# Scan of a four-block model: one saturating add for two state groups, odd groups decayed by GpSimd, block diagonal tables loaded from memory

## The reference, cut to what matters

```
xr, gate = split(x @ W_in.T, 2)                  # 512 channels each
xc = silu(causal_conv(xr + t_emb))               # 4 taps
xn = layernorm(xc) * ln_g + ln_b
Bm, Cm, dt = split(xn @ W_xproj.T, 3)            # 16 states each
Ad = 1 + tanh(dt @ W_dt.T + b_dt) * 0.01 * -tanh(A_log)
Bd = Bm * min(norm(xn), 1)
def step(h, (ad, bd, xt, ct)):                   # h: 16 x 512 for each sequence
    h = clip(h * ad[:, :, None] + bd[:, :, None] * xt[:, None, :], -10, 10)
    return h, einsum('bd,bdh->bh', ct, h)        # y_t
y = scan over the 64 tokens + D * xn
out = (y * silu(gate)) @ W_out.T
```

## Time and profile before

| | |
|---|---|
| median of 3 runs | 1796.69 us (1794.53 to 1799.46) |
| the profiled execution's own time | 1796.37 us |
| its span | 1794.6 us |
| DVE, PE busy | 1623.4 us (90%), 1636.4 us (91%) |
| ACT, POOL busy | 1297.0 us (72%), 622.6 us (35%) |
| attention, both layers | up to about 550 us |
| layer 1: front, scan, post | about 550 to 745, 745 to 1094, 1094 to 1180 us |
| layer 2: scan, post | 1370 to 1718, 1718 to 1794.6 us |

### The profile page before, as it was taken

One profiled execution on the slowest core, in us unless ns is written; L12 is line 12 of the kernel. 1 busy time (PEld: TensorE's weight loads), 2 busy tenths in 40 slices (PEclk: granted clock), 3 DMA queues, 4 the chain that ended last, 5 costly groups with the idle time before them and its releaser, 6 DMA issues. The chain is left out here.

```text
span 1794.6 us, 42356 instructions
## 1 busy us (share of the span) xinstructions
PE 1636.4 (91%) x13764; PEld 703.6 (39%) x13764; DVE 1623.4 (90%) x2452; ACT 1297.0 (72%) x2197; POOL 622.6 (35%) x576
## 2 busy tenths in 40 slices
PE   7999999999999999788888889999997888888898
PEld 3555555555554445222111114544452221111144
DVE  5899999999987999889999998679998899999975
ACT  5655556465646999888999993069897899999910
POOL 0223232232330222265665550002223566555500
PEclk9999999999999999899999999999998999999999
DMA  4000000000002344653555667624345545556668
GB/s 162 1 2 0 1 2 31 2 1 0 1 1 83 139 160 152 192 171 120 183 160 188 218 186 210 229 83 174 127 169 173 178 132 183 158 187 197 189 224 280
DMA packets 126444, 226.56 MB, mean 126 GB/s; under 512 B 35616, under 2 KB 61216, under 8 KB 117536
## 3 DMA queue, kind: packets, MB, share of 16 engines
q1 hardware_dynamic: 125904, 223.30, 37.8%
q10 hardware_dynamic: 432, 1.84, 0.3%
HBM read 141.73 MB, written 83.36 MB: 125 GB/s over the span
## 5 line engine op out<-in xcount | busy, mean ns | idle before, releaser
L1038 ACT ACTIVATE R<-q,Ast 128x512 f32<-128x512 f32 x1008 | 627.2, 708 | 21.8 <-DVE q L2018 16.6
L2018 DVE CUSTOM_DVE_ANT_0 q<-R,PS 128x512 f32<-128x512 f32 x1008 | 611.2, 677 | 19.7 <-ACT R L1038 9.3
L1479 PE MATMUL PS<-xq,Uw 96*128 96x512 bf16 x1024 | 346.2, 394 | 87.5 <-DVE q L2018 73.2
L613 POOL TENSOR_TENSOR Uw<-Ub,rowmask 96x512 bf16<-96x512 bf16 x256 | 335.8, 1346 | 254.4 <-PE PS L1479 254.4
L1492 PE MATMUL PS<-q,Wy 128*32 128x512 f32 x2048 | 285.2, 620 | 0.3
L1479 PEld LDWEIGHTS PS<-xq,Uw 96*128 96x128 bf16 x1024 | 85.5, 97 | 473.9 <-DVE q L2018 396.0
L1152 PE MATMUL PS<-X,Win 128*128 (+1 forms) x456 | 214.7, 608 | 2.2 <-issue 2.1
L1053 PE MATMUL PS<-xn,Wl 128*128 128x512 f32 x384 | 187.7, 613 | 0.7 <-DVE xn L1605 0.7
L1723 DVE SCALAR_TENSOR_TENSOR acc<-xp,Wc,acc 128x512 f32<-128x512 f32 x192 | 134.5, 748 | 2.6
L547 POOL TENSOR_TENSOR ex<-ex,rs 128x1024 f32<-128x1024 f32 x32 | 76.8, 2401 | 164.2 <-DVE rs L1628 164.2
L1152 PEld LDWEIGHTS PS<-X,Win 128*128 128x128 f32 x456 | 82.5, 191 | 95.8 <-issue 95.1
(11 more groups left out here) (159 smaller groups left out, 2492.6 us busy)
## 6 DMA issues: line engine op xcount, KB each, us to landing
xq<-xpart_d SPq DMA_DIRECT2D x384, 192.0 KB
sg_d<-sg SPq DMA_DIRECT2D x16, 1024.0 KB, 5.0
xn_d<-z SPq DMA_DIRECT2D x16, 1024.0 KB, 3.9
y_d<-ys SPq DMA_DIRECT2D x64, 256.0 KB, 3.8
xnp<-xn_d SPq DMA_DIRECT2D x16, 1024.0 KB, 8.1
sgp<-sg_d SPq DMA_DIRECT2D x16, 1024.0 KB, 11.2
xpart_d<-xh SPq DMA_DIRECT2D x16, 512.0 KB, 2.9
xpart_d<-xmi SPq DMA_DIRECT2D x16, 512.0 KB, 3.8
```

The costliest lines, as they stand in the source:

```text
L613: pl.tensor_tensor(Uw[0:XROWS, h, w, :, :, :], Ub[0:XROWS, w, 0:N, ds(s0, CH)].rearrange("p n t -> p t n").unsqueeze(2).broadcast_to([XROW ...
L1038: act.activation(R[:, w, :], q[:, (t + 1) % 2, w, :], ACT.Copy, scale=Ast[:, h, w, t:t + 1]).then_inc(ac_r, 1)
L1479: pe.matmul(PS[:, w, :], Uw[0:XROWS, h, w, t, :, :].rearrange("p b n -> p (b n)"), xq[0:XROWS, hb, w, s8 % XT, :], start=True, stop=True). ...
L2018: v._custom_dve(bass.dve_ops.TENSOR_ADD_SAT, out=q[:, s8 % 2, w, :], in0=R[:, w, :], in1=PS[:, w, :], s0=CLIP, s1=-CLIP).then_inc(dv_q, 1)
```

## The change

Seven edits are made together.

1. **One add for two groups.** DVE's `step` runs over p = 0, 1 and adds groups 2p and 2p + 1 in one 128 x 1024 instruction over two PSUM banks.
2. **Odd groups decayed by GpSimd.** ACT decays the even groups; GpSimd the odd ones, with `tensor_scalar` (`odd_decay`). The add waits for both.
3. **y copies on ScalarE.** `keep_y` leaves DVE for ACT.
4. **B tables from memory.** The three parts of B are stored into `bdiag_d`, a table in memory that was filled with zeros once (12 DMAs of 256 KB in the attention stage), at such offsets that it is block diagonal. `load_x` gets a fourth DMA that brings `Uw` for two steps. GpSimd's `stage` products, `Ub`, `rowmask`, the rows of ones, nine table loads and the table memsets go. K is 72.
5. **B turned in the front.** `store_b` needs tokens on partitions, so PE transposes rB (`turn_b`) and DVE's `split_b` reads it from PSUM.
6. **GpSimd's `last_parts` waits later**: for `row_r` instead of `rB_r`, that is behind DVE's L1860.
7. In the tail the middle part of x goes to ACT (`last_middle`), the low part to GpSimd in halves (`last_half`).

```diff
-                def split_b(it):
+                def split_b(it, src):
                     v.wait_ge(tv_st, it * (TV_STORES * 16) + TV_STORES * 16)
-                    v.wait_ge(rB_r, it + 1)
+                    v.wait_ge(bt_mm, it + 1)
...
                 def step(pi, c2, s8, first):
                     n = c2 * 8 + s8
-                    for w in range(QW):
-                        v.wait_ge(pe_w, pi * (QW * S) + n * QW + w + 1 + W0)
-                        if w % 2 == 0:
-                            v.wait_ge(pe_yq, pi * (2 * S) + n * 2 - 4 + w // 2 + 1 + USED)
...
+                    for p in range(2):
+                        state = q[:, s8 % 2, 2 * p:2 * p + 2, :].rearrange("p w c -> p (w c)")
+                        fed = PS[:, 2 * p:2 * p + 2, :].rearrange("p w c -> p (w c)")
+                        v.wait_ge(pe_w, pi * (QW * S) + n * QW + 2 * p + 2 + W0)
+                        v.wait_ge(pe_yq, pi * (2 * S) + n * 2 - 4 + p + 1 + USED)
...
+                        v.wait_ge(pd_r, pi * RS + n * 2 - 2 + p + 1 + READY)
+                        v.wait_ge(ac_r, pi * RS + n * 2 - 2 + p + 1 + READY)
                         alone(v)
-                        v._custom_dve(bass.dve_ops.TENSOR_ADD_SAT, out=q[:, s8 % 2, w, :], in0=R[:, w, :], in1=PS[:, w, :],
+                        v._custom_dve(bass.dve_ops.TENSOR_ADD_SAT, out=state, in0=R[:, 2 * p:2 * p + 2, :].rearrange("p w c -> p (w c)"), in1=fed,
                                       s0=CLIP, s1=-CLIP).then_inc(dv_q, 1)
...
+                def odd_decay(pi, c2, s8, p):
+                    h, t = s8 // CH, s8 % CH
+                    if t < 2 and p == 0:
+                        pl.wait_ge(pl_a, pi * CHUNKS + c2 * 2 + h + 1)
+                    pl.wait_ge(dv_q, pi * (2 * S) + c2 * 16 + 2 * s8 + p + 1)
+                    alone(pl)
+                    pl.tensor_scalar(R[:, 2 * p + 1, :], q[:, (t + 1) % 2, 2 * p + 1, :], Ast[:, h, 2 * p + 1, t:t + 1], None,
+                                     ALU.mult).then_inc(pd_r, 1)
...
                 def load_x(ps, k):
+                    rows = bdiag_d[ps, 0:GB * DIAG].rearrange("(r f) -> r f", f=S * ROW)
+                    sp.dma_start(Uw[0:XROWS, k % XB, :, :, :, :].rearrange("p t w b n -> p (t w b n)"),
+                                 rows[:, k * (XT * ROW):(k + 1) * (XT * ROW)].unsqueeze(0)
+                                 .broadcast_to([PARTS, GB * PARTS, XT * ROW])).then_inc(xq_in[k % XB], 16)
...
-                    pl.wait_ge(rB_r, it + 1)
+                    pl.wait_ge(row_r, it * 2 + (2 * AT + 3))
...
+                def keep_y(pi, ck, h):
+                    act.wait_ge(pe_yq, pi * (2 * S) + ck * (2 * CH) + 2 * CH + USED)
+                    act.wait_ge(y_out[h], pi * (CHUNKS // 2 * 16) + (ck - h) * 8 + 16)
+                    alone(act)
+                    act.activation(ys[:, h, :], PS[:, 4 + h, :], ACT.Copy).then_inc(ac_y, 1)
...
+                def turn_b(it, dst):
+                    pe.wait_ge(rB_r, it + 1)
+                    pe.transpose(dst, rB[:, :], ident[:, :]).then_inc(bt_mm, 1)
```

More of the change, by code:

```diff
@@ L184, in cond_resid_kernel @@
         late = ExitStack()
+        sb("table_gap", [P, TT * DI + P], where=late)
         pass_tables.append(tables(1, late))
@@ new lines, in last_half, with last_group @@
+                def last_half(it, k, b):
+                    if b == 0:
+                        pl.wait_ge(xmi_r, it * TT + k + 1)
+                        alone(pl)
+                    cols = slice(b * (DI // 2), (b + 1) * (DI // 2))
+                    low = pl.tensor_tensor(xlo[:, k, cols], xr1[:, k, cols], xmi[:, k, cols], ALU.subtract)
+                    if b:
+                        low.then_inc(xlo_r, 1)
+                def last_group(n, p):
+                    it = l * G + G - 1
+                    if n == 19 and p == 0:
+                        pl.wait_ge(xq_st, it * 48 + 48)
+                        alone(pl)
+                    for k, at in enumerate((20, 22, 23, 25)):
+                        if n == at:
+                            last_half(it, k, p)
@@ new lines, in eight @@
+                def eight(ps, c2, first=False, last=False, tail=False):
+                    pi = l * PASSES + ps
+                    for s8 in range(8):
+                        for p in range(2):
+                            if not (first and s8 == 0):
+                                odd_decay(pi, c2, s8, p)
+                            if tail:
+                                last_group(c2 * 8 + s8, p)
+                        if s8 == 0:
+                            if not first:
+                                stage_decay(ps, c2, 1)
+                        elif s8 == 1:
+                            if not first:
+                                stage_outputs(ps, c2, 1)
+                        elif s8 == 4 and not last:
+                            stage_decay(ps, c2 + 1, 0)
+                        elif s8 == 5 and not last:
+                            stage_outputs(ps, c2 + 1, 0)
+                        elif s8 == 5 and ps + 1 < PASSES:
+                            pl.wait_ge(tab_in[1], l * (16 * TABLES) + 16 * TABLES)
+                            alone(pl)
+                            stage_decay(ps + 1, 0, 0, True)
+                            stage_outputs(ps + 1, 0, 0)
+                        elif s8 == 7 and last and ps + 1 < PASSES:
+                            stage_decay(ps + 1, 0, 1, True)
+                            stage_outputs(ps + 1, 0, 1)
```

289 lines of the change are left out of this document (118 added, 171 removed).

## The result

The changed kernel takes 1984.58 us in the median (1970.3 to 1991.09), the kernel before 1796.54 on the same chip: a ratio of 1.1038 with a 95% interval of 1.0995 to 1.1082. It is slower by 188 us, far outside the predicted range of 1728 to 1806, and it went the way of rival B. The profiled execution took 1987.97 us, its span is 1986.2, 191.6 more than before.

The account below looks back on a forecast made before the run. DVE was taken as the bound, ACT nearly full; afterwards PE's loop at 2.51 us a step. Gains of 6 in steady steps, 13 in tails and 3 in front gave 1796.4 - 22 = 1774 us, range 1728 to 1806.

Parts of the forecast that it names:

- rival B: Scan loop add, decay, add: slower by GpSimd's decay, deciding from 0.85 us a decay; about 1850 with 1.16; chance 0.15.
- the price of GpSimd's decay: Scan, odd groups: a decay taken at 0.65 us, nearer to the one-input cast (0.62) than the two-input difference (1.16).
- The loop around the decay: Scan, same pair: add 1.22, hop to GpSimd 0.18, decay, some 0.3 of waits; 1.70 + 0.65 = 2.35 us a step.
- hidden: GpSimd's load in the scan, 1.3 us a step of decays plus 0.15 for staging, was to cost no time.
- rival A: Scan steps: DVE stays the bound or nearly, 2.28 to 2.43 us a step, 1722 to 1757; chance 0.25.
- the sum: Whole kernel: gains of 6 (steady steps), 13 (tails) and 3 (front), 22 us off 1796.4, giving 1774.
- at nothing: Fourth DMA of `load_x` and other side edits: no cost; queue 3.3 us in 5.0, DMA share about 0.7.
- The wide add: DVE in the scan: one 128x1024 add lasts about 1.22 us, pairs start 1.14 apart, a step 2.28.
- PE's loop of 2.51: Hardware loops: PE's order makes a loop over two steps, 4.57 + 0.45 = 5.02, so 2.51 us a step.
- the waits in front of the add: Hardware loops, between PE's input matmul and DVE's add: 0.45 us, bounds 0.21 and 0.55.
- The tails: 24 tail steps of each layer: 76 us instead of 82.8, a gain of 6.5 a layer, 13 in all.
- The front: Bodies before the scan: L1860 falls from 1.28 to 0.35 us, 0.2 a body, 3 us over 14.

Follow-up runs that it names:

- e3: Changed kernel with only group 3 decayed by GpSimd, groups 0 to 2 by ACT; 1958.0 us, ratio 1.090.
- e4: Changed kernel with GpSimd's decay written as a product of two tensors; 1895.0 us, ratio 1.055.
- n1: Changed kernel with all decays on ACT, y copies on DVE and one narrow add a group; 1890.4 us, ratio 1.052.
- b2: Changed kernel with table loads as three DMAs of 24 rows of 4 KB for every two halves, with their own semaphore; 1978.4 us, ratio 1.105.
- n2: Kernel before with one wide add a pair of groups and nothing else changed; 1862.5 us, ratio 1.035.
- f1: n1 with each half's table load as three DMAs of 24 rows of 2 KB, three halves ahead; 1821.8 us, ratio 1.014.
- n3: Changed kernel with GpSimd's decay cut to 64 of 512 columns, the other 448 left undecayed (timing only); 1891.8 us, ratio 1.050.
- b3: n3 with the table loads of b2 (timing only); 1812.7 us, ratio 1.011.
- b4: Changed kernel with b2's table loads and each odd group's decay shared: ACT columns 0 to 191, GpSimd the rest as a product of two tensors; 1840.5 us.
- f2: b4's shared decay split at column 128 (ACT 128 columns, GpSimd 384), with f1's table loads; 1820.9 us, ratio 1.012.
- g1: f1 with last-pass gate and y loads issued one by one, y copies on ACT, columns 256 to 511 of group 3 decayed by GpSimd; 1794.9 us.

## Why the prediction was wrong

**The failed step is the price of GpSimd's decay**, "a decay has one tensor input and a scalar for each partition, which is nearer to the cast, so I take 0.65", with the bounds 0.62 and 1.16. It is 1.56. Both bounds came from other operations of that width, and the upper one was no bound: an operation with a scalar for each partition that the trace did not show cost a third more than the dearest one it did. What rival B's text quotes for one-input work on GpSimd doesn't hold for this form: the cast of this width takes 0.62. The loop around the decay was right to 0.01 us: 1.70 + 1.56 = 3.26, and e3, in which GpSimd is half idle, measured 3.25; for e4 the same sum gives 2.74, measured 2.67. The price also undoes the sentence that GpSimd's load is "hidden": 2 x 1.56 and 0.15 for staging fill 3.25 us by themselves, which in the changed kernel happens to equal the loop. With the true price the prediction's own sum says 208 x (3.25 - 2.54) = 148 us more in the steady steps. Rival B had the place, the mechanism and the point from which it decides (0.85), but its chance of 0.15 and its far end of 1850 hung on the same wrong bound. (In rival A's sum the upper gain is 54 + 16 = 70, not 75.)

**The clock was not in the sum.** The scans grew by 192.6, of which 148 is the step. Most of the other 45 lies where TensorE was at 1.2 GHz, as read from the places where steps are longer than 3.25; no run isolates it. From 1550 to 1830 us that is two thirds of the time, and there PE can fill the step by itself. The starts of two steps in a row from that stretch, 3.68 us apart:

```profile
1702.97 2.35 DVE L2045 CUSTOM_DVE_ANT_0 q<-R,PS 128x1024 f32<-128x1024 f32 x2 [1.32 <-PE PS L1502]
1706.65 2.35 DVE L2045 CUSTOM_DVE_ANT_0 q<-R,PS 128x1024 f32<-128x1024 f32 x2 [1.33 <-PE PS L1502]
```

Between them PE's inputs start at 1705.41, 1.87 after y, and the next y at 1707.22, 1.81 after the inputs: no pause is left. At 2.4 GHz, in the changed kernel, PE pauses some 1.2 us a step (0.94 and 0.31 in front of its inputs of 1001.76 and 1003.67). What pause exactly makes the clock fall isn't settled: from 995 to 1124 us the same steps ran at 2.4 GHz. In e4 and n1 it fell behind waits for transfers, in b2 without any; n2, with pauses of 0.6 us, kept 1.00.

**The loads "at nothing" were wrong in themselves, but cost the changed kernel next to nothing** (b2: 6 us). SP's issue time was right (0.76 + 2.42 for the four) and the DMA share was near (0.7 foretold; 0.69 in f1). What was missed is the form of the table load (69 us from n1 to f1), by all that is seen how its rows are spread over the engines. Had the decay been cheap, this would have been the failure: n1 and n3 stand at 1.05.

**Two steps of the sum held.** The wide add is 1.22 us. PE's loop of 2.51 is 2.47 in b3 (the waits in front of the add 0.40, predicted 0.45), so rival A's 2.28 did not come even with a cheap decay. **The tails** would have shrunk as said: in b3 the first 46 wide adds stand so,

```profile
L2052 DVE CUSTOM_DVE_ANT_0 q<-R,PS x46: 1208/1214/1222, 748.9 to 820.2; 128x1024 f32<-128x1024 f32 x46
```

71.3 us from the first start to the last. In the kernel before the same point is the start of the 91st add, 76.8 us after the first (749.9 to 826.7). That is 5.5 us less, predicted 6.5 for each layer. With the real decay they grew: the 46th add of the changed kernel starts at 831.4, 82.2 after its first.

**The front**: L1860, now L1885, fell to 0.35 in all sixteen, as said:

```profile
L1885 DVE SCALAR_TENSOR_TENSOR rows<-middle,masks,remain x16: 350/352/353, 560.1 to 1450.0; 128x128 bf16<-128x128 bf16 x16
```

The scan starts 0.7 us earlier for seven bodies, 0.1 a body where 0.2 was predicted.

**The rest of the 2.54 that seemed free was never large.** The wide add lowers DVE's load but makes the dependent chain longer, by one add's second half and by both decays. With the decays shared between ACT and GpSimd, b4 and f2 come to 2.51 and 2.49, and their late loads cost more than that. Only g1, which leaves the adds narrow and takes work off ACT and DVE evenly, shortens the step by more than 0.1, to 2.39.

## What to carry to other kernels

In a recurrence, cost a wider instruction by the loop it stands in (its own length, everything serial between its end and its next start), and by its engine's load as well: e3 had GpSimd half idle and the same step, the changed kernel had both at 3.25. An operation that the trace doesn't show has no upper bound from its neighbours; time it alone first, here the bound was off by a third and the forecast by some 210 us. When one cause is mended and little comes back (b2: 6 us), mend the other one too before judging: the four corners 1984.6, 1978.4, 1891.8 and 1812.7 say what no single edit says.
